# Convolution on 64x64 blocks of TensorE, in a sequence that mixes long and short blocks

## The chip, the cores and the metric

One core of one Trainium2 chip runs the whole program. The metric is the device time in microseconds (us) of one execution; the kernel before takes 877.8 us (median of 3 runs, 876.87 to 878.94).

## The reference, cut to what matters

The input `x` is [32 batches, 64 channels, 1024 features]. The program adds to it an attention block fed by a causal long convolution, and then a feed-forward block with low-rank experts. Only the convolution is touched, and the weights of the layer behind it:

```python
u_m    = u * mask                         # positions at or past length[batch] are zero
kernel = _get_kernel(log_dt, C, ...)      # [64 channels, 1024 positions]
y = irfft(rfft(u_m) * rfft(kernel))[..., :1024] + u_m * D
y = y * mask
# then q, k, v = y @ Wq.T, y @ Wk.T, y @ Wv.T ...
```

So for each channel, `y[b, t] = sum over s <= t of kernel[t - s] * x[b, s]`. The kernel of a channel comes from products of two small tables (a row index and a column index of 32 each), which TensorE forms in groups of eight channels.

## The kernel before, in words

**The convolution as matrix products.** The 1024 positions of a channel are 8 tiles of 128, or 16 blocks of 64. A row-shifted copy of the channel's kernel, the Toeplitz operand `toep`, lies with 64 partitions per channel and L + 64 = 1088 columns; any 64 of its columns are the 64x64 block that carries inputs over one distance. Two channels are worked on at once, one in partitions 0 to 63 and one in 64 to 127: a "pair", and there are 32 pairs (`for n in range(S // 2)` in `conv_matmuls`). The inputs of a pair, `xc`, hold for each tile the two 64-row halves; 32 batches are the columns, so a product over k tiles has 32k columns.

`convolve` (line 668) issues for each distance d in tiles and each input half c one product. `wide` (line 644) does it on the 64x128 form of the array: 64 rows of contraction, all 128 output positions, one instruction for each channel of the pair. `narrow` (line 655) does the same with two 64x64 products, one for each 64-row half of the output. Nine of sixteen (d, c) are wide in even pairs and eight in odd ones; wide and narrow runs are laid so that two narrow runs meet. In tile distance 0 the late input half also meets the early output half; that block of `toep` is all zero and is multiplied too. All operands are float32, for which each product shows as two records in the trace.

Products of a pair go to two PSUM banks of a ring of three pairs. VectorE multiplies them with the mask (line 740), ScalarE rounds to the high part `y_hi` (lines 771, 772), GpSimd subtracts for the low part `y_lo` (lines 783, 784).

**The loads.** The Toeplitz operand is read from the scratch `kpad` in DRAM by four DMAs for each pair (line 606: two channels, two halves of the columns) into a ring of three buffers. The load for pair n waits until pair n-3 has been multiplied (line 617), the inputs of pairs n, n+1 for the same (line 593, two DMAs every second pair, issued ahead of the Toeplitz loads). All of these sit in one in-order queue, SyncE's (`conv_loads`, line 625). In the same queue `conv_loads` puts one quarter of a weight block behind each of the loads of pairs 5 to 16: two blocks of the value weights and the first block of the key weights (line 642).

**The group kernels.** Every four pairs `kernels_pe` (line 536) makes the kernels of the eight channels of a later group: four 64x128 products of 128 columns. VectorE adds the two row halves (line 561 and following), ScalarE's queue stores them to `kpad` (line 573).

**The splits of the weights.** At pairs 15 and 19 ScalarE makes the high parts of the value weights and of the first key weights (line 820), and GpSimd their low parts at pairs 15, 19 and 23 (lines 824, 828).

**What follows.** The value products (line 952) come first; their first half needs only the first 16 pairs. Then the key and query products (line 988), attention, and the feed-forward block.

Of the kernel before, what the change touches and what calls it, by code (L numbers as in the profile page):

```python
# [14 lines left out]
P = 128  # L15
# [19 lines left out]
HB = 32  # L35
# [29 lines left out]
def constants():  # L65

    t = np.zeros((P, NCONST), np.float32)

    def put(name, v):
        at, n = CONSTS[name]  # L70
        t[:, at:at + n] = v

    p = np.arange(P)
    put("ident", np.eye(P))
    inv_freq = (1.0 / np.float32(10000.0) ** (np.arange(0, HD, 2, dtype=np.float32) / HD)).astype(np.float32)
    freqs = np.outer(np.arange(S, dtype=np.float32), inv_freq).astype(np.float32)
# [6 lines left out]
    put("pos", p[:, None] + P * np.arange(NJ)[None, :])  # L83
# [18 lines left out]
def build(nc, x_conv, x_nat, lens, cond, modes, d_skip,  # L102
          w_qk, w_v, w_o, w_cond, w_ffn, w_b, consts, out):
    ctx = ExitStack()
    with ctx:
# [26 lines left out]
        WR = 3  # L132
        W_FIRST = 6
        wraw = sb("wraw", [P, WR, NJ * P], F32, s12)
# [3 lines left out]
        TR = 3  # L138
        toep = sb("toep", [P, TR, L + HALF], F32, s1)
        XH, XR = 2, 2  # L140
# [409 lines left out]
        def kernels_out(v, g):  # L550
            v.wait_ge(pe_k, step_of(g) + 1)
            if g == 2:
                for pair in range(GP):
                    v.wait_ge(st_first[pair], 16 * 2)
            if g > 2:
                for pair in range(XH):
                    v.wait_ge(st_k[g % 2 * XH + pair], stored_before(g - 2))
            k = ksb[:, g % 2, :, :]
            low = ps[:, 6, 0:GC].rearrange("p (u b) -> p u b", u=2)
            high = ps[:, 7, 0:GC].rearrange("p (u b) -> p u b", u=2)  # L560
# [5 lines left out]
            v.tensor_tensor(k0, k0, along(d_at[:, g, :], GP), ALU.add).then_inc(v_k, 1)  # L566

        def store_kernels(eng, g):
            eng.wait_ge(v_k, step_of(g) + 1)
            heads = kpad.ap()[g * HGRP:(g + 1) * HGRP, P - 1:P - 1 + L].rearrange("(u k) (a b) -> k a u b", u=2, b=HB)  # L570
            for pair in range(XH):
                for k in (pair, XH + pair):
                    eng.dma_start(heads[k], ksb[k * HB:(k + 1) * HB, g % 2, :, k * HB:(k + 1) * HB])\
                       .then_inc(st_k[g % 2 * XH + pair], 16)
# [19 lines left out]

        FIRST_ROWS = [(0, 2 * P + HALF), (2 * P + HALF, NJ // 2 * P + HALF), (NJ // 2 * P + HALF, L + HALF)]

        ROW_HALVES = [(0, (L + HALF) // 2), ((L + HALF) // 2, L + HALF)]

# [6 lines left out]
        def load_rows(eng, n, r, lo, hi, landed):  # L605
            eng.dma_start(toep[r * HALF:(r + 1) * HALF, n % TR, lo:hi],  # L606
                          bass.AP(kpad, head(n, r) * (KROW + 1) + lo, [[1, HALF], [1, hi - lo]])).then_inc(landed, 16)

# [13 lines left out]
        W_PIECES = 4  # L622
        W_COLS = NJ * P // W_PIECES

        def conv_loads(sp):
# [4 lines left out]
            for n in range(1, S // 2):  # L630
# [6 lines left out]
                load_toeplitz(sp, n)  # L637
                part, piece = divmod(n - W_FIRST + 1, W_PIECES)
                if 0 <= part < 3:
                    cols = slice(piece * W_COLS, (piece + 1) * W_COLS)  # L640
                    source = w_v[:, part * NJ * P:(part + 1) * NJ * P] if part < 2 else w_qk[0]
                    sp.dma_start(wraw[:, part, cols], source[:, cols]).then_inc(ld_w[part // 2 * 2], 16)

        def wide(pe, n, c, d, start, stop=False):

            at = d * P + (1 - c) * HALF
            for r in range(2):
                rows = slice(r * HALF, (r + 1) * HALF)
                mm = pe.matmul(ps[:, 2 * (n % 3) + r, d * NB:NJ * NB], toep[rows, n % TR, at:at + P],  # L649
                               xc[rows, n // XH % XR, 1 - c, n % XH, 0:(NJ - d) * NB],  # L650
                               start=start, stop=stop)
            return mm

        def narrow(pe, n, c, d, start, stop=False):

            for half in range(2):
                at = d * P + (1 + half - c) * HALF
                for r in range(2):
                    rows = slice(r * HALF, (r + 1) * HALF)
                    mm = pe.matmul(ps[half * HALF:(half + 1) * HALF, 2 * (n % 3) + r, d * NB:NJ * NB], toep[rows, n % TR, at:at + HALF],  # L660
                                   xc[rows, n // XH % XR, 1 - c, n % XH, 0:(NJ - d) * NB],
                                   start=start, stop=stop)
            return mm

        TILES = [(d, c) for d in range(NJ) for c in range(2)]
        WIDE, NARROW = TILES[:NJ + 1], TILES[NJ + 1:]

        def convolve(pe, n):
# [6 lines left out]
            else:  # L675
                pe.wait_ge(ld_toep[n % TR], rows_landed(n))
            if n % 2 == 0:
                for d, c in WIDE:
                    if n == 0 and (d, c) == (2, 0):
                        pe.wait_ge(ld_mid, 16 * 2)  # L680
                    if n == 0 and (d, c) == (4, 0):
                        pe.wait_ge(ld_toep[0], 16 * 2)
                    mm = wide(pe, n, c, d, start=((d, c) == WIDE[0]))
                for d, c in NARROW:
                    mm = narrow(pe, n, c, d, start=False, stop=((d, c) == NARROW[-1]))
            else:
                for d, c in [WIDE[0]] + NARROW:
                    mm = narrow(pe, n, c, d, start=((d, c) == WIDE[0]))
                if n == 1:
                    kernels_pe(pe, 1)  # L690
                for d, c in WIDE[1:]:
                    mm = wide(pe, n, c, d, start=False, stop=((d, c) == WIDE[-1]))
            mm.then_inc(pe_conv, 1)
# [60 lines left out]
        def conv_hi(act):  # L754
# [4 lines left out]
            for n in range(S // 2):  # L759
# [4 lines left out]
                if n % GP == 0 and 0 < g < NHG - 1:  # L764
                    store_kernels(act, g + 1)
                if n == W_FIRST + 9:
                    weight_hi(act, -1)
                if n == W_FIRST + 13:
                    weight_hi(act, 0)
                act.wait_ge(v_mask, n + 1)  # L770
# [5 lines left out]
        def conv_lo(gp):  # L776
            exponents(gp, 1)
            for n in range(S // 2):
# [5 lines left out]
                gp.tensor_tensor(y_pair(1, n, 1), ym_pair(n, 1), y_pair(0, n, 1).bitcast(F32), ALU.subtract).then_inc(g_ylo, 1)  # L784
                if n == W_FIRST + 9:
                    value_weight_lo(gp, 0)
                if n == W_FIRST + 13:
                    value_weight_lo(gp, 1).then_inc(g_wlo, 1)
                if n == W_FIRST + 17:
                    weight_lo(gp, 0)  # L790

# [5 lines left out]
        def w_loaded(eng, m):  # L797

            s = w_slot(m).start
            pieces = (2 * W_PIECES, 0, W_PIECES)[s]  # L800
            whole = 0 if m <= 0 else (m - 1) // WR + 1 if s == 0 else m // WR + (s == 1)
            eng.wait_ge(ld_w[s], 16 * (pieces + whole))

# [4 lines left out]
        def load_weights(sp, m):  # L808
# [4 lines left out]
            s = w_slot(m).start  # L813
            sp.dma_start(wraw[:, s, :], w_qk[m]).then_inc(ld_w[s], 16)

# [67 lines left out]

        def qkv_transfers(sp):
            load_weights(sp, 1)
            load_weights(sp, 2)
# [115 lines left out]
        def qkv_hi(act):  # L1002
            act.wait_ge(g_ylo, S // 2)
            for n in range(4 * NU):
                if next_weights(n) is not None:
# [68 lines left out]

        def qkv_rope_sin(gp):
            for n in range(4 * NU):
                if next_weights(n) is not None:
# [836 lines left out]
```

## Time and profile before

| what | us |
|---|---|
| median of 3 runs | 877.8 |
| the profiled execution itself | 876.56 |
| its span | 874.7 |
| PE busy in it | 854.1 (98%) |
| products at line 649 (wide), busy | 97.1 |
| first product of the convolution starts | 20.55 |
| first value product starts | 164.40 |

The span is the time from the first to the last instruction; the profiled execution is 1.86 us longer than it. PE is TensorE's matmuls, PEld its weight loads, which run beside them. SPq is SyncE's queue while it issues DMAs. The granted clock is 1.00 in all 40 slices of the profile.

### The profile page before, as it was taken

What the parts mean: (1) busy time and instruction counts of PE and PEld (TensorE: products, weight loads), DVE (VectorE), ACT (ScalarE), POOL (GpSimd) and SP (SyncE); (2) the same over time, 40 slices, a digit from 0 to 9 for tenths busy, and PEclk for the clock granted to TensorE, in tenths of its full rate; (3) what the DMA queues carried; (4) which work ended last, traced back from release to release, by engine and by line L of the source; (5) the groups of instructions that cost most, each with busy time, mean ns of one, the idle gap of its engine ahead of it and who ended that gap; (6) DMA issues with size and microseconds to landing.
All of it is one profiled execution on the core that took longest, in us unless ns stands there. A gap on an engine that the chain in (4) does not pass through costs nothing.

```text
span 874.7 us, 24616 instructions
## 1 busy us (share of the span) xinstructions
PE 854.1 (98%) x10866; PEld 741.9 (85%) x10866; DVE 467.1 (53%) x898; ACT 221.4 (25%) x377; POOL 450.0 (51%) x346
## 2 busy tenths in 40 slices
PE   3999999999999999999999999999999999999998
PEld 2899999988888888887777777777779999999998
DVE  7555651122522222238887777888854755545444
ACT  4445552100000000013132333333334322211220
POOL 3344555302367555649978888877746422102220
PEclk9999999999999999999999999999999999999999
DMA  3788877413354322255534454545437211222211
GB/s 95 177 207 220 208 186 196 162 60 127 109 183 129 82 74 73 50 166 154 142 129 149 135 176 165 173 163 173 151 123 234 96 59 57 83 97 97 98 49 49
DMA packets 97339, 114.90 MB, mean 131 GB/s; under 512 B 44112, under 2 KB 66896, under 8 KB 97232
## 3 DMA queue, kind: packets, MB, share of 16 engines
q1 hardware_dynamic: 94240, 112.29, 43.1%
q8 instruction: 86, 1.41, 0.7%
q10 hardware_dynamic: 2480, 0.51, 0.3%
q0 software_dynamic: 512, 0.53, 0.2%
q14 instruction: 21, 0.17, 0.1%
HBM read 80.16 MB, written 33.13 MB: 130 GB/s over the span
## 4 chain that ended last, share of the span: by engine, by line
PE 93%; SPq 3%; DMA 2%; DVE 1%; issue 0%; ACT 0%
PE ps L988 25%; PE ps L1275 21%; PE ps L1597 15%; PE ps L649 8%; PE ps L1625 5%; PE ps L952 5%; PE ps L660 4%; PE ps L1231 3%; PE ps L1211 3%; PE ps L1507 2%; SPq L606 2%; DMA toep<-kpad 2%; PE ps L1642 1%; PE ps L1641 1%; DMA kpad<-ksb 1%
## 5 line engine op out<-in xcount | busy, mean ns | idle before, releaser
L1597 PE MATMUL ps<-wb_hi,xf 128*128 128x424 f32 x440 | 127.0, 356 | 0.0
L988 PE MATMUL ps<-y_hi,w_hi 128*128 128x512 f32 x320 | 125.1, 391 | 0.0
L988 PE MATMUL ps<-y_hi,w_lo 128*128 128x512 f32 x320 | 124.5, 389 | 0.0
L988 PE MATMUL ps<-y_lo,w_hi 128*128 128x512 f32 x320 | 124.5, 389 | 0.0
L1573 POOL TENSOR_TENSOR xf<-xs,xf 128x512 fp32r<-128x512 f32 x32 | 42.1, 1347 | 124.8 <-DVE xs L1561 124.8
L1275 PE MATMUL ps<-y_hi 128*128 128x512 f32 x256 | 102.9, 402 | 0.0
L1275 PE MATMUL ps<-y_hi,y_lo 128*128 128x512 f32 x256 | 100.2, 391 | 0.0
L1275 PE MATMUL ps<-y_lo,y_hi 128*128 128x512 f32 x256 | 100.1, 391 | 0.0
L649 PE MATMUL ps<-xc,toep 64*128 64x192 f32 (+4 forms) x1088 | 97.1, 330 | 2.5 <-DMA toep<-kpad 2.4
L649 PEld LDWEIGHTS ps<-xc,toep 64*128 64x128 f32 x1088 | 91.2, 187 | 6.0 <-issue 3.8
L1597 PEld LDWEIGHTS ps<-wb_hi,xf 128*128 128x128 f32 x440 | 82.7, 188 | 2.3
L1100 POOL TENSOR_TENSOR rot<-rot,cst 128x512 f32<-128x512 f32 x40 | 52.8, 1319 | 58.7 <-DVE rot L1070 58.7
L1303 POOL TENSOR_TENSOR sc<-sc,stat 128x1024 f32<-128x1024 f32 x32 | 62.0, 1937 | 38.8 <-DVE stat L1299 38.8
L1597 PE MATMUL ps<-wb_lo,xf 128*128 128x424 f32 x220 | 77.6, 353 | 0.0
L1070 DVE LOAD_MASK_SELECT rot<-ps x40 | 0.6, 14 | 134.1 <-PE ps L988 119.1
L988 PEld LDWEIGHTS ps<-y_hi,w_hi 128*128 128x128 f32 x320 | 60.1, 188 | 12.8
L988 PEld LDWEIGHTS ps<-y_hi,w_lo 128*128 128x128 f32 x320 | 60.1, 188 | 12.5
L988 PEld LDWEIGHTS ps<-y_lo,w_hi 128*128 128x128 f32 x320 | 60.1, 188 | 12.3
L1317 POOL TENSOR_TENSOR sc<-sc,stat 128x1024 f32<-128x1024 f32 x32 | 66.8, 2086 | 2.2 <-DVE stat L1313 2.2
L783 POOL TENSOR_TENSOR y_lo<-ym,y_hi 128x256 fp32r<-128x256 f32 x32 | 30.3, 946 | 70.0 <-ACT y_hi L772 69.8
L1104 POOL TENSOR_TENSOR rf<-rot,rc 128x512 f32<-128x512 f32 x40 | 52.7, 1317 | 17.2 <-DMA k_rows<-rf 14.1
L820 ACT ACTIVATE w_hi<-wraw 128x1024 fp32r<-128x1024 f32 (+1 forms) x11 | 12.4, 1137 | 186.6 <-PE ps L988 108.8
(190 smaller groups left out, 1624.3 us busy)
## 6 DMA issues: line engine op xcount, KB each, us to landing
toep<-kpad SPq DMA_DIRECT2D x124, 136.0 KB
xc<-in_dram SPq DMA_DIRECT2D x32, 256.0 KB, 4.4
q_rows<-rf SPq DMA_DIRECT2D x32, 256.0 KB, 2.8
q<-q_rows SPq DMA_DIRECT2D x16, 512.0 KB, 3.9
xr<-in_dram SPq DMA_DIRECT2D x16, 512.0 KB, 4.4
x_scratch<-xr SPq DMA_DIRECT2D x16, 512.0 KB, 3.0
x<-x_scratch SPq DMA_DIRECT2D x16, 512.0 KB, 4.3
out_dram<-x SPq DMA_DIRECT2D x15, 512.0 KB, 2.9
```

Of the source, the lines that this page charges most:

```text
L649: mm = pe.matmul(ps[:, 2 * (n % 3) + r, d * NB:NJ * NB], toep[rows, n % TR, at:at + P], xc[rows, n // XH % XR, 1 - c, n % XH, 0:(NJ - d) * ...
L660: mm = pe.matmul(ps[half * HALF:(half + 1) * HALF, 2 * (n % 3) + r, d * NB:NJ * NB], toep[rows, n % TR, at:at + HALF], xc[rows, n // XH % ...
L952: mm = pe.matmul(out, wv[a][:, j, h * P:(h + 1) * P], y[b][:, j, b0:b1, s0:s1], start=(j == 0 and a + b == 0), stop=(j == NJ - 1 and a == 1))
L988: mm = pe.matmul(kq_bank(n), w[a][:, j, :], yt[b][:, j, g * 512:(g + 1) * 512], start=(j == 0 and a + b == 0), stop=(j == NJ - 1 and a == 1))
L1100: gp.tensor_tensor(r, r, across(C("sin"), 8), ALU.mult).then_inc(g_rsin, 1)
L1104: gp.tensor_tensor(rf[:, (NVB + n) % SR, :], rot[:, n % RR, :], rc[:, n % RR, :], ALU.add).then_inc(g_rsum, 1)
L1275: mm = pe.matmul(ps[:, 6 + n, :], heads, wo(c, t)[:, n, :], start=(at == 0), stop=(at == 3 * NQT - 1))
L1303: gp.tensor_tensor(sc_groups(u), sc_groups(u), along(stat[:, u % CR, 0, :], S), ALU.subtract).then_inc(g_sub, 1)
L1317: gp.tensor_tensor(sc_groups(u), sc_groups(u), along(stat[:, u % CR, 2, :], S), ALU.mult).then_inc(g_prob, 1)
L1573: gp.tensor_tensor(xf(i, op, 1)[:], xs(i, op), xf(i, op, 0)[:].bitcast(F32), ALU.subtract).then_inc(g_xflo, 1)
L1597: mm = pe.matmul(dst[:, PLAIN:], xf(i, idx, a)[:, t, :], wb(c, idx, t), start=(start and t == 0 and a + c == 0), stop=(t == 3 and a == 1), ...
L1625: mm = pe.matmul(plain_bank[:, k, :], xf(i, op, a)[:, t, :], w[c][:, first + t, :], start=(op in (A11, S1) and t + a + c == 0), stop=(op i ...
```

## The change

- `toeplitz_block` takes the place of `wide` and `narrow`: every product is 64x64, with at most 128 columns. Output tiles 0 to 3 and 4 to 7 are separate segments (`seg`). In segment 1 the two 64-row halves of the output tiles are exchanged: `side` 0 holds the late half. A block is (side, segment, distance in 64s); the blocks of the zero corner are not issued. There are 46 blocks for each channel of a pair, in place of 9 wide and 14 narrow ones in even pairs, 8 wide and 16 narrow ones in odd pairs.
- The sequence of a pair is `MIXED_ORDER`: distance 0 of both segments, then for far = 1 to 7 the blocks of segment 1 at distance far (128 columns), of segment 0 at 8 - far and of segment 1 at 16 - far, and last distance 8. Pair 0 goes by rising distance.
- The Toeplitz operand has 1024 columns in place of 1088, and its loads accordingly.
- `kernels_pe` makes only the diagonal blocks that are used: eight 64x64 products of 64 columns, and VectorE's three operations on them are half as wide.
- The mask's positions and the weights' rows follow the exchanged halves: half of each weight block is loaded with its partition halves exchanged. A weight load in the layer behind is three DMAs in place of one.
- The value weights' first block is loaded in four pieces behind pairs 5, 8, 11, 14, its second in four pieces of two DMAs behind pairs 17, 20, 23, 26; they are split at pairs 27 and 29. The first key weights are loaded and split behind the convolution.

```diff
-        toep = sb("toep", [P, TR, L + HALF], F32, s1)
+        toep = sb("toep", [P, TR, L], F32, s1)
@@ kernels_pe
             for u in range(2):
-                cols = slice(u * P, (u + 1) * P)
-                for r in range(2):
-                    rows = slice(r * HALF, (r + 1) * HALF)
-                    mm = pe.matmul(ps[:, 6 + r, cols], ltab[rows, cols], rtab[rows, cols], start=True, stop=True)
+                for half in range(2):
+                    cols = slice(u * P + half * HALF, u * P + (half + 1) * HALF)
+                    for r in range(2):
+                        rows = slice(r * HALF, (r + 1) * HALF)
+                        mm = pe.matmul(ps[half * HALF:(half + 1) * HALF, 6 + r, u * HALF:(u + 1) * HALF], ltab[rows, cols], rtab[rows, cols],
+                                       start=True, stop=True)
@@ convolution
-        def wide(pe, n, c, d, start, stop=False):
-        def narrow(pe, n, c, d, start, stop=False):
+        def toeplitz_block(pe, n, at, start, stop):
+            side, seg, dist = at
+            late = side if seg == 0 else 1 - side
+            c = (late - dist) % 2
+            shift = (dist + c - late) // 2
+            lo, hi = max(seg * NJ // 2, shift), (seg + 1) * NJ // 2
             for r in range(2):
                 rows = slice(r * HALF, (r + 1) * HALF)
+                mm = pe.matmul(ps[side * HALF:(side + 1) * HALF, 2 * (n % 3) + r, lo * NB:hi * NB], toep[rows, n % TR, dist * HALF:(dist + 1) * HALF],
+                               xc[rows, n // XH % XR, 1 - c, n % XH, (lo - shift) * NB:(hi - shift) * NB],
                                start=start, stop=stop)
             return mm
+        def reach(side, seg):
+            return (seg + 1) * NJ - 2 + (side if seg == 0 else 1 - side)
+        def both_sides(seg, dist):
+            return [(side, seg, dist) for side in range(2) if dist <= reach(side, seg)]
+        BY_DISTANCE = [at for dist in range(NDIST) for seg in (1, 0) for at in both_sides(seg, dist)]
+        MIXED_ORDER = both_sides(1, 0) + both_sides(0, 0)
+        for far, small in zip(range(1, NJ), range(NJ - 1, 0, -1)):
+            MIXED_ORDER += both_sides(1, far) + both_sides(0, small) + both_sides(1, small + NJ)
+        MIXED_ORDER += both_sides(1, NJ)
@@ load_weights
-            sp.dma_start(wraw[:, s, :], w_qk[m]).then_inc(ld_w[s], 16)
+            near, far = slice(0, NJ // 2 * P), slice(NJ // 2 * P, NJ * P)
+            sp.dma_start(wraw[:, s, near], w_qk[m][:, near]).then_inc(ld_w[s], 16)
+            sp.dma_start(wraw[0:HALF, s, far], w_qk[m][HALF:P, far]).then_inc(ld_w[s], 16)
+            sp.dma_start(wraw[HALF:P, s, far], w_qk[m][0:HALF, far]).then_inc(ld_w[s], 16)
```

## Rows read from the trace of the kernel before

**Rows 1.** The page's first part: busy time, share, instructions of each engine.
```profile
PE 854.1 (98%) x10866; PEld 741.9 (85%) x10866; DVE 467.1 (53%) x898; ACT 221.4 (25%) x377; POOL 450.0 (51%) x346
```

**Rows 2.** Windows by stage: length, busy time by engine, granted clock, DMA share, GB/s.
```profile
36.20:95.00 58.80, 57.76 (x1268) 54.63 (x1261) 31.20 (x66) 30.63 (x51) 29.20 (x34) 1.00 0.91 218
95.00:164.40 69.40, 69.18 (x1522) 65.70 (x1521) 27.09 (x51) 27.43 (x47) 38.88 (x39) 1.00 0.72 187
```

**Rows 3.** The chain in order of time (start, length, what): two pairs in mid-convolution.
```profile
83.14 5.90 PE ps L649 x68
89.03 2.59 PE ps L660 x120
91.63 2.80 PE ps L649 x32
```

**Rows 4.** Windows over line 660 alone: length, PE busy (records), PEld, clock, DMA.
```profile
80.47:81.30 0.83, 0.82 (x40) 0.82 (x44) 1.00 1.08 235
80.47:81.51 1.04, 1.03 (x56) 1.03 (x60) 1.00 1.09 234
```

**Rows 5.** Groups by line and form: count, busy us, mean ns of one.
```profile
L660 PE MATMUL ps<-xc,toep 64*64 64x96 f32 x512 | 16.4, 243 | 0.0
...
L660 PE MATMUL ps<-xc,toep 64*64 64x64 f32 x512 | 13.2, 218 | 0.0
...
L660 PE MATMUL ps<-xc,toep 64*64 64x32 f32 x512 | 12.4, 212 | 0.0
```

**Rows 6.** The chain in order of time: three places where a Toeplitz load ends last.
```profile
27.92 3.83 DMA toep<-kpad
...
31.89 3.31 PE ps L649 x36
...
63.26 4.70 DMA toep<-kpad
...
138.44 0.63 SPq L593
...
139.83 0.55 SPq L606
...
141.71 5.21 DMA toep<-kpad
...
147.05 3.31 PE ps L649 x36
```

**Rows 7.** TensorE's timeline: pairs 3, 4 and 10, and their idle time before.
```profile
40.42 0.61 PE L543 MATMUL ps<-ph 64*128 64x128 f32 x8
41.14 3.31 PE L649 MATMUL ps<-xc,toep 64*128 64x256 f32 x36
...
55.40 2.87 PE L649 MATMUL ps<-xc,toep 64*128 64x256 f32 x32
...
68.09 3.31 PE L649 MATMUL ps<-xc,toep 64*128 64x256 f32 x36 [0.93 <-DMA toep<-kpad]
```

**Rows 8.** SyncE's timeline: issues in the convolution and behind it.
```profile
53.80 0.57 SPq L642 DMA_DIRECT2D wraw<-in_dram  x1
...
129.56 1.29 SPq L593 DMA_DIRECT2D xc<-in_dram  x2
130.95 6.86 SPq L606 DMA_DIRECT2D toep<-kpad  x8
```

**Rows 9.** GpSimd's timeline: a weight split, the last low parts, the first key split.
```profile
115.87 2.38 POOL L824 TENSOR_TENSOR w_lo<-wraw,w_hi 128x1024 fp32r<-128x1024 f32 x1
...
166.34 0.90 POOL L783 TENSOR_TENSOR y_lo<-ym,y_hi 128x256 fp32r<-128x256 f32 x1 [2.45 <-ACT y_hi L772]
167.18 0.91 POOL L784 TENSOR_TENSOR y_lo<-ym,y_hi 128x256 fp32r<-128x256 f32 x1
```

**Rows 10.** The whole chain in order of time: value products, key and query products.
```profile
164.40 44.37 PE ps L952 x240
208.77 179.52 PE ps L988 x792
```

More of the change, by code:

```diff
@@ L82, in constants @@
     put("causal", np.where(q < k, np.finfo(np.float32).min, np.float32(0)))
-    put("pos", p[:, None] + P * np.arange(NJ)[None, :])
+    turned = np.arange(NJ)[None, :] >= NJ // 2
+    put("pos", np.where(turned, (p[:, None] + HALF) % P, p[:, None]) + P * np.arange(NJ)[None, :])
     put("step", np.arange(HB)[None, :])
@@ L132, in build @@
         WR = 3
-        W_FIRST = 6
+        W_FIRST, W_EVERY = 5, 3
         wraw = sb("wraw", [P, WR, NJ * P], F32, s12)
@@ L557, in kernels_out @@
                     v.wait_ge(st_k[g % 2 * XH + pair], stored_before(g - 2))
-            k = ksb[:, g % 2, :, :]
-            low = ps[:, 6, 0:GC].rearrange("p (u b) -> p u b", u=2)
-            high = ps[:, 7, 0:GC].rearrange("p (u b) -> p u b", u=2)
+            k = ksb[:, g % 2, :, 0:HALF]
+            low = ps[:, 6, 0:P].rearrange("p (u b) -> p u b", u=2)
+            high = ps[:, 7, 0:P].rearrange("p (u b) -> p u b", u=2)
             v.tensor_copy(k, low).then_inc(v_kl, 1)
@@ L565, in kernels_out @@
             k0 = k.rearrange("p u (i b) -> p u i b", b=HB)[:, :, :, 0]
-            v.tensor_tensor(k0, k0, along(d_at[:, g, :], GP), ALU.add).then_inc(v_k, 1)
+            v.tensor_tensor(k0, k0, along(d_at[:, g, :], 2), ALU.add).then_inc(v_k, 1)
         def store_kernels(eng, g):
@@ L572, in store_kernels @@
                 for k in (pair, XH + pair):
-                    eng.dma_start(heads[k], ksb[k * HB:(k + 1) * HB, g % 2, :, k * HB:(k + 1) * HB])\
+                    eng.dma_start(heads[k], ksb[k * HB:(k + 1) * HB, g % 2, :, k % 2 * HB:(k % 2 + 1) * HB])\
                        .then_inc(st_k[g % 2 * XH + pair], 16)
@@ L593, in load_x_conv @@
                 sp.dma_start(xc[r * HALF:(r + 1) * HALF, t % XR, :, :, :], halves[:, :, first:first + XH, :]).then_inc(ld_xc[t % XR], 16)
-        FIRST_ROWS = [(0, 2 * P + HALF), (2 * P + HALF, NJ // 2 * P + HALF), (NJ // 2 * P + HALF, L + HALF)]
-        ROW_HALVES = [(0, (L + HALF) // 2), ((L + HALF) // 2, L + HALF)]
+        FIRST_ROWS = [(0, 2 * P), (2 * P, NJ // 2 * P), (NJ // 2 * P, L)]
+        ROW_HALVES = [(0, L // 2), (L // 2, L)]
         def rows_landed(n):
@@ L623, in build @@
         W_COLS = NJ * P // W_PIECES
+        W_SPLIT = 27
         def conv_loads(sp):
@@ L637, in conv_loads @@
                 load_toeplitz(sp, n)
-                part, piece = divmod(n - W_FIRST + 1, W_PIECES)
-                if 0 <= part < 3:
+                part, piece = divmod((n - W_FIRST) // W_EVERY, W_PIECES)
+                if n >= W_FIRST and (n - W_FIRST) % W_EVERY == 0 and part < 2:
                     cols = slice(piece * W_COLS, (piece + 1) * W_COLS)
-                    source = w_v[:, part * NJ * P:(part + 1) * NJ * P] if part < 2 else w_qk[0]
-                    sp.dma_start(wraw[:, part, cols], source[:, cols]).then_inc(ld_w[part // 2 * 2], 16)
@@ L644, in wide @@
-        def wide(pe, n, c, d, start, stop=False):
-            at = d * P + (1 - c) * HALF
+                    rows = w_v[:, part * NJ * P:(part + 1) * NJ * P]
+                    if part == 0:
+                        sp.dma_start(wraw[:, 0, cols], rows[:, cols]).then_inc(ld_w[0], 16)
+                    else:
+                        sp.dma_start(wraw[0:HALF, 1, cols], rows[HALF:P, cols]).then_inc(ld_w[0], 16)
+                        sp.dma_start(wraw[HALF:P, 1, cols], rows[0:HALF, cols]).then_inc(ld_w[0], 16)
@@ L651, in wide @@
                                start=start, stop=stop)
             return mm
-        def narrow(pe, n, c, d, start, stop=False):
[L656 to L663, printed above, removed]
@@ L665, in build @@
-        TILES = [(d, c) for d in range(NJ) for c in range(2)]
-        WIDE, NARROW = TILES[:NJ + 1], TILES[NJ + 1:]
+        NDIST = 2 * NJ
+        def reach(side, seg):
[4 more added lines that the diff above has]
+        MIXED_ORDER = both_sides(1, 0) + both_sides(0, 0)
@@ L676, in convolve @@
                 pe.wait_ge(ld_toep[n % TR], rows_landed(n))
[L677 to L689, printed above, removed]
+            order = BY_DISTANCE if n == 0 else MIXED_ORDER
+            for k, at in enumerate(order):
+                if n == 0 and at == (0, 1, 4):
+                    pe.wait_ge(ld_mid, 16 * 2)
+                if n == 0 and at == (0, 1, 8):
+                    pe.wait_ge(ld_toep[0], 16 * 2)
+                if n == 1 and k == len(order) // 2:
                     kernels_pe(pe, 1)
-                for d, c in WIDE[1:]:
-                    mm = wide(pe, n, c, d, start=False, stop=((d, c) == WIDE[-1]))
+                last = all(other[0] != at[0] for other in order[k + 1:])
+                mm = toeplitz_block(pe, n, at, start=(at[1:] == (1, 0)), stop=last)
             mm.then_inc(pe_conv, 1)
@@ L765, in conv_hi @@
                     store_kernels(act, g + 1)
-                if n == W_FIRST + 9:
+                if n == W_SPLIT:
                     weight_hi(act, -1)
-                if n == W_FIRST + 13:
-                    weight_hi(act, 0)
                 act.wait_ge(v_mask, n + 1)
@@ L784, in conv_lo @@
                 gp.tensor_tensor(y_pair(1, n, 1), ym_pair(n, 1), y_pair(0, n, 1).bitcast(F32), ALU.subtract).then_inc(g_ylo, 1)
-                if n == W_FIRST + 9:
+                if n == W_SPLIT:
                     value_weight_lo(gp, 0)
-                if n == W_FIRST + 13:
+                if n == W_SPLIT + 2:
                     value_weight_lo(gp, 1).then_inc(g_wlo, 1)
-                if n == W_FIRST + 17:
-                    weight_lo(gp, 0)
         NU = NG + NQT
@@ L799, in w_loaded @@
             s = w_slot(m).start
-            pieces = (2 * W_PIECES, 0, W_PIECES)[s]
-            whole = 0 if m <= 0 else (m - 1) // WR + 1 if s == 0 else m // WR + (s == 1)
-            eng.wait_ge(ld_w[s], 16 * (pieces + whole))
+            pieces = 3 * W_PIECES if s == 0 else 0
+            whole = 0 if m < 0 else (m - 1) // WR + 1 if s == 0 else m // WR + 1
+            eng.wait_ge(ld_w[s], 16 * (pieces + 3 * whole))
         def w_users(m):
@@ L884, in qkv_transfers @@
         def qkv_transfers(sp):
+            load_weights(sp, 0)
             load_weights(sp, 1)
@@ L1003, in qkv_hi @@
             act.wait_ge(g_ylo, S // 2)
+            weight_hi(act, 0)
             for n in range(4 * NU):
@@ L1075, in qkv_rope_sin @@
         def qkv_rope_sin(gp):
+            weight_lo(gp, 0)
             for n in range(4 * NU):
```

4 lines of the change are left out of this document (1 added, 3 removed).

## The prediction

> **What bounds the kernel now.** Read the page's first part first: TensorE is busy 98% of the span [rows 1], no other engine over 53%. Then the chain in order of time: the value, key and query products stand in it unbroken for 44.37 and 179.52 us [rows 10], so nothing but their own length sets that stage. The change doesn't touch them; what it can win or lose lies before 164.40, where the first value product starts. There TensorE is busy for 57.76 of 58.80 and 69.18 of 69.40 us [rows 2], so the convolution is bound by its products. But the chain shows a second candidate close behind: in three places it runs through the Toeplitz loads (3.83, 4.70, 5.21 us from the last issue to the landing) [rows 6], and TensorE sat idle 0.93 us before pair 10 [rows 7]. The DMA share is 0.91 at 218 GB/s up to 95 us [rows 2]. So two limits lie within a few per cent of each other, and the sum has to be made for both.
>
> **The change, part by part.**
>
> *Length of a pair, before.* Two pairs are one wide run of 68 records (5.90 us) and one narrow run of 120 (2.59 us): 8.49, that is 4.245 us a pair [rows 3]. Columns: wide, even pair 2x256 + 2x224 + 2x192 + 2x160 + 128 = 1792, odd 256 less, 3328 for both; narrow 512 and 768, 1280 for both. That is 2304 a pair. A record streams a column in about 0.83 ns: the 64x96 record is 25 ns longer than the 64x64 one [rows 5], 0.78 ns a column, and two cycles at 2.4 GHz (granted clock 1.00, the upper level, in all stretches [rows 2]) are 0.83. With two records for a product: 2304 x 1.667 = 3.84 us. The other 0.405 us is overhead: changing between the 64x128 and the 64x64 form, a little at each round, and short rounds.
>
> *Length of a pair, after.* Both sides of the array have 2176 columns (side 0: 10x128 + 2x96 + 2x64 + 2x32 = 1664 in segment 1 and 512 in segment 0; side 1: 1536 and 640). So 2176 x 1.667 = 3.63 us. Records a pair: 46 x 2 channels x 2 = 184, before 94 on average (34 wide and 60 narrow).
> The price of more records is read from one narrow run [rows 4]. Its first 40 records (10 rounds of four: 128, 128, 4x96, 4x64 columns, 896 in all) took 0.83 us against 0.747 by columns; part of the 0.08 is the entry. Rounds down to 64 columns thus cost little over their columns. The next 16 records (four rounds of 32 columns) took 0.21 us, 52 ns a round against 27 by columns. Rows 5 say the same: from 64 to 32 columns the record shortens by 6 ns only. So a long round hides the next weight load and a 32-column round doesn't.
> Now the bounds. Below: 46 rounds' worth at 2.5 ns each is 0.12, nothing else, 3.75 us. Above: if the two sides have to go in step, each group costs its wider side, 2304 columns again, 3.84 + 0.12, and its eight 32-column rounds cost 25 ns more each, 0.20: 4.16. The old overhead by round gives about the same: 0.405 us over 32 rounds is 12.7 ns, by 46 rounds 0.58, so 4.21. I take 3.9: the sequence puts at most four short rounds behind two long ones, which is the pattern that was cheap, and no form is changed any more; the sides' differences (32 against 64, then 64 against 32) mostly meet again in the next group.
> The Trainium skill speaks to this twice, and the pages differ. "TensorEngine Tiling (Array Packing)", Key Properties, has tiles operate independently and a mode switch drain the array, which gives the low end. "TensorE: Matmul & The Clock Gate", Part 3, says matmuls start and end strictly in program order; two sides of unequal width would then wait for each other, which gives the upper figure (rival B). No run of before has unequal sides, so the trace decides neither.
>
> *Group kernels.* 8 records of 0.61 us with the neighbours' overlap, between the pairs [rows 7]; after, half the columns in each quadrant: about 0.3 us. Per four pairs that is 0.3 less on TensorE, if TensorE is the limit. VectorE's narrower additions save nothing: its share is 0.53 [rows 2].
>
> *The load path.* The load for pair n may start when pair n-3 is done. For even n, SyncE issues two input loads (1.29 us) and four Toeplitz loads at about 0.64 each [rows 8]; the last of these is issued 3.3 us after the end of pair n-3, and lands 3.83 to 5.21 us on [rows 6]: 7.2 to 8.6 us, with 0.14 to the start. Measured whole at pair 28: 138.44 to 147.05, 8.6 us; at pair 10, with the queue behind on weight pieces, 58.3 to 68.09, 9.8 us [rows 6, 7]. For odd n the 1.3 us of inputs fall away, so they aren't the limit. Call it L. If an even pair waits for its load, then start(n) = end(n-3) + L, the pair n-4 starts two pair lengths before end(n-3), and four pairs take 2T + L. With T = 4.245 that was 8.49 + 8.2 = 16.7 against 4T + 0.5 = 17.5: the load path was hidden. With T = 3.9 it is 7.8 + 8.2 = 16.0 against 4T + 0.3 = 15.9: the two limits meet, and the load path is the next wait. I take L = 8.2, above the middle, since the transfers come more densely: a pair moves 0.79 MB of operands (0.82 before), and with kernels and weights some 0.85 MB in 4.0 us, 212 GB/s, where before had 218 at a share of 0.91 [rows 2].
> The weights help a little: eight groups of pieces over 22 pairs in place of twelve behind pairs 5 to 16; each piece costs SyncE 0.57 us [rows 8]. Behind pairs 17, 20, 23, 26 two pieces are 1.2 us; the odd pair's load behind it has more room than that.
>
> *The start.* Pair 2 starts at 31.89 on a load that SyncE's queue set [rows 6], not the products; that stays. Pair 4 started at 41.14 [rows 7]; now two pairs and the kernels later 31.89 + 7.8 + 0.3 = 40.0, its own load at about 40.4. I take 40.4.
>
> *The end of the convolution.* GpSimd splits value weights behind pair 29: 2.38 us [rows 9]. Low parts end 3.7 us after their pair (167.18 + 0.91 against 164.40), so this split ends 6.1 us after pair 29's end, 1.7 before the value products begin at 7.8; pair 30's low part comes 0.4 us late, pair 31's not at all. Cost nothing; if ScalarE were late with the high part, up to 2 us. Behind the value products' 44.37 us [rows 10] there is room for loading and splitting the first key weights (three DMAs, about 2 us of issue). The two DMAs more in each later weight load are 1.3 us of SyncE for four products of 5.4 us; the chain there holds no load at all [rows 10].
>
> *The sum.* Pairs 4 to 31 are 28 pairs of 16.0/4 = 4.0 us: 40.4 + 112 = 152.4. The value products start 12.0 us earlier, and the rest follows unchanged. The profiled execution's 876.56 becomes 864.6. It stood 1.2 under the median of 877.8, so the median to expect is 865.8.
>
> **The rivals.**
> B, *the sides go in step*: T = 4.16, four pairs max(8.3 + 8.2, 16.6 + 0.3) = 16.9, the 28 pairs 118.5; the start at 40.6 gives 159.1, 5.3 us gained: 872.5. For it: nothing in the trace shows unequal sides at the same time. Against it: the wide runs keep going while the two channels are skewed, so strictly common rounds aren't needed there.
> A, *the load path takes it back*: L = 9.8 as at pair 10 [rows 7]; four pairs 17.6, the 28 pairs 123: 163.6, so 877.0. For it: a DMA share of 0.91 where L was longest [rows 2]. Against: the pair 10 case had a weight piece behind every pair, and total bytes fall.
> C, *slower: weight loads come bare*. If the mixture breaks the hiding and each round pays the 25 ns of a 32-column round [rows 4], T = 3.63 + 46 x 0.0275 = 4.9; 28 pairs are 139.3, to 180 us: 893. It decides from T = 4.35 on, 15 ns a round. For it: twice the records. Against it: the ten long rounds of rows 4 paid 8 ns at most, the entry included, and only 8 of 46 groups have 32 columns.
> D, *the exchange of the halves gains no column* (2304 after all, but short rounds as cheap as in the forecast): T = 3.84 + 0.12 = 3.96, four pairs 16.1, 28 pairs 113: 866.7. It lies inside the forecast's range, because the load path is the limit by then.
>
> **How the numbers follow.** The forecast's mechanism (T from 3.75 to 4.0, L from 7.5 to 8.6; 859 to 869) has 0.68; B 0.13, D 0.01 beyond the forecast's own values; A 0.12, of which most ends between 869 and 876; C 0.04; a new wait behind the convolution 0.02. The low end, T = 3.75 and L = 7.3: four pairs 15.3, 107 us, 147.4: 860.8; a little below that for an L under 7.2. The range that leaves out 2 in 10 is 860.5 to 872.5. A change of under 0.2% (1.8 us) can't be told from none. Faster than that: 0.93; within: 0.03; slower: 0.04.
>
> **What would show it.** The wide form gone; records at the new line 32x184 = 5888 in number; pair starts 3.9 to 4.0 apart; TensorE's idle time before even pairs grown from a few tenths to some us in all, released by the Toeplitz loads; the first value product at 152.4; the 44.37 and 179.5 us behind it unchanged. I am wrong if the records run without idle time at over 4.1 us a pair (B, C), if idle time takes over 10 us (A), or if idle time appears behind the convolution.

## The result, and the profile after

The changed kernel takes 934.9 us (median of 4 runs, 933.3 to 939.6) against 878.4 us: 1.0655 times as long, 95% interval 1.0625 to 1.0686. The forecast was 865.8, range 860.5 to 872.5. It was wrong in sign.

The profiled execution has a span of 932.0 us. Its page, first the busy time of each engine (before: [rows 1]), then TensorE's busy tenths in 40 slices, then the queue by which instructions arrive:

```profile
span 932.0 us, 30510 instructions
PE 860.3 (92%) x13802; PEld 746.9 (80%) x13802; DVE 466.6 (50%) x898; ACT 221.4 (24%) x377; POOL 449.1 (48%) x346
...
PE   3776776679999999999999999999999999999998
...
q8 instruction: 109, 1.79, 0.8%
```

TensorE has 2936 more matmul records and only 6.2 us more of busy time. Its share is 6 or 7 tenths in slices 1 to 8, where it was 9. The last row (packets, MB, share of 16 engines) is the one to learn to read: 109 packets, 1.79 MB, so 16.4 KB each. The program has 2 x 13802 matmuls and weight loads; 27604 by 109 is 253, so one packet is a block of about 256 instructions, 128 records with their weight loads. The same row of the kernel before:

```profile
q8 instruction: 86, 1.41, 0.7%
```

The row doesn't name the engine that a packet is for, but the difference does: the counts of the other engines hardly moved, and 2936 more TensorE records came with 23 more packets, 128 records for each.

And the same queue in the window from 20 to 165 us alone, in the convolution, of the kernel before and then of the changed one:

```profile
q8 instruction: 25, 0.41, 1.3%
```

```profile
q8 instruction: 34, 0.56, 1.7%
```

One block per 5.8 us before, one per 4.26 us after: 145 us by 25 and by 34. The packet itself is short: 1.7% of 16 engines in 145 us is 39 us for 34 packets, an estimate of 1.2 us for each.

Where the idle time is, and what ended it: the waits of TensorE in the convolution (idle us, times, longest), then its timeline from pair 4 on (start, length, what, records, idle before).

```profile
PE ps L661 <- issue: 52.9, 43, 2.2
PE ps L661 <- DMA toep<-kpad: 0.3, 1, 0.3
```

```profile
45.96 2.85 PE L661 MATMUL ps<-xc,toep 64*64 64x128 f32 x128 [0.34 <-issue]
50.51 3.11 PE L661 MATMUL ps<-xc,toep 64*64 64x96 f32 x127 [1.70 <-issue]
54.44 3.28 PE L661 MATMUL ps<-xc,toep 64*64 64x128 f32 x128 [0.82 <-issue]
58.65 2.96 PE L661 MATMUL ps<-xc,toep 64*64 64x32 f32 x128 [0.93 <-issue]
63.75 3.04 PE L661 MATMUL ps<-xc,toep 64*64 64x128 f32 x127 [2.14 <-issue]
```

Nothing that the profile shows was waited for ("issue"), the operand loads were in time (0.3 us in all), and the stops come every 128 records nearly throughout (43 stops; the convolution has 46 times 128 records), whatever block of the sequence stands there: before a product of 128, 96 or 32 columns, in the middle of a pair. A pair has 184 records, so these stops don't belong to pairs; the work between two of them is that of one packet of instructions.

The trace also has the start and the length of each packet of this queue, and they tie the two together. Each of the 43 stops ended 1.2 to 1.7 us (median 1.46) after such a packet had landed, and the next packet started 1.0 to 2.6 us (median 1.74) after TensorE had resumed; the packet itself took 1.1 us. 1.46 + 1.74 + 1.11 is 4.3 us: a chain of one packet at a time, not a full transfer path.

The whole convolution (count, shortest, median and longest record, first and last start):

```profile
L661 PE MATMUL ps<-xc,toep x5888: 186/269/471, 20.9 to 220.2; 64*64 64x128 f32 x91, 64*64 64x32 f32 x37, 64*64 64x96 f32 x35, 64*64 64x64 f32 x34
```

With the 112 records of the group kernels that is 6000 records in 199.3 us: 4.25 us for 128. Per pair 6.2 us, where the forecast had 4.0.

Behind it the chain in order of time answers [rows 10]:

```profile
220.49 44.34 PE ps L960 x240
264.84 179.52 PE ps L996 x792
```

The value products start 56.1 us later than before (220.49 against 164.40), and the lengths of both stages are the same. The span grew by 57.3 us; the other 1.2 us lie in the attention, where the chain shows two more stops released by nothing shown ("issue", 0.37 us at 536.0 and 0.75 at 639.7); the interval from tile to tile, 7.4 us elsewhere, is 8.2 and 8.4 there, and the kernel before had two smaller ones of this sort.

### The profile page after: what moved, and what is told of

Its sections match the earlier page's. It is cut to its first block, busy times and chain, and to the rows that moved or that the text cites. A ratio compares the mean times of both kernels' runs of the same rounds, so it can differ in the third digit from the quotient of the medians.

```text
span 932.0 us, 30510 instructions
## 1 busy us (share of the span) xinstructions
PE 860.3 (92%) x13802; PEld 746.9 (80%) x13802; DVE 466.6 (50%) x898; ACT 221.4 (24%) x377; POOL 449.1 (48%) x346
## 3 DMA queue, kind: packets, MB, share of 16 engines
q8 instruction: 109, 1.79, 0.8%
## 4 chain that ended last, share of the span: by engine, by line
PE 91%; issue 6%; DVE 1%; DMA 1%; SPq 1%; ACT 0%
PE ps L996 23%; PE ps L1285 19%; PE ps L661 15%; PE ps L1607 14%; PE ps L1635 5%; PE ps L960 5%; PE ps L1241 3%; PE ps L1221 3%; PE ps L1517 2%; PE ps L1652 1%; PE ps L1651 1%; SPq L609 1%; DMA kpad<-ksb 1%; DMA toep<-kpad 0%; PE ps L1619 0%
## 5 line engine op out<-in xcount | busy, mean ns | idle before, releaser
L661 PE MATMUL ps<-xc,toep 64*64 64x128 f32 (+3 forms) x5888 | 146.3, 253 | 53.2 <-issue 52.9
L661 PEld LDWEIGHTS ps<-xc,toep 64*64 64x64 f32 x5888 | 137.1, 138 | 61.6 <-issue 61.6
L748 DVE TENSOR_TENSOR ym<-ps,valid 128x512 f32<-128x512 f32 x32 | 22.1, 692 | 125.0 <-PE ps L661 124.9
```

The source lines that it names most:

```text
L661: mm = pe.matmul(ps[side * HALF:(side + 1) * HALF, 2 * (n % 3) + r, lo * NB:hi * NB], toep[rows, n % TR, dist * HALF:(dist + 1) * HALF], x ...
```

## The experiments

Two theories. **F**: TensorE is fed its instructions in blocks of 256, one about every 4.3 us at best, and 184 records a pair ask for more. **S**: the sequence is itself slow, by bare weight loads, by sides that wait for each other, or by the order. The kernel before ran beside all of them (877 to 879 us).

**Same count, fewer columns.** In the changed kernel:

```diff
             lo, hi = max(seg * NJ // 2, shift), (seg + 1) * NJ // 2
+            if dist > 0:
+                lo = hi - 1
```

> The changed kernel with every 64x64 product but those of distance 0 cut to its last 32 columns: the same 184 records a pair, about a third of the columns (the rest of the convolution's sum is left out). Theory F (TensorE is fed one 16 KB block of instructions, 128 records with their weight loads, about every 4.3 us): the count decides, so the convolution keeps 46 blocks x 4.3 = about 200 us and the run 925 to 937 us. Theory S (the products themselves, or weight loads laid bare, are slower in the mixed sequence): the convolution falls to the floor of short rounds, 46 rounds x 2 x 0.058 = 2.7 us of work a pair, then bound by the loads at about 4 us: 860 to 870 us.

Measured: 933.1 us. The products of this run, in the same view:

```profile
L663 PE MATMUL ps<-xc,toep x5888: 186/291/473, 20.9 to 219.6; 64*64 64x32 f32 x181, 64*64 64x128 f32 x16
```

And the granted clock by slices of its page:

```profile
PEclk9776777559999999999999999999999999999999
```

Of the 4352 columns of a pair (both sides) 1856 are left, 57% went, and the convolution is 0.6 us shorter: 4.24 us for 128 records. The time goes with the count, not with the columns. The run is less clean than it looks, since the granted clock was lower in most of this stretch (0.50 to 0.83 by windows of 20 us) and the records took longer for it; but TensorE still stood for 44.6 us in 32 stops that nothing shown released, and each ended 1.3 to 1.7 us after an instruction packet had landed. Together with the bare length of a pair further down, S is out as the cause of the 56 us.

**No Toeplitz loads** from pair 3 on:

```diff
-                load_toeplitz(sp, n)
+                if n < TR:
+                    load_toeplitz(sp, n)
+                else:
+                    sp.wait_ge(pe_conv, n - TR + 1)
```

> The changed kernel with no Toeplitz loads from pair 3 on; the products read the three buffers that are there (so the convolution's values are those of the first three pairs' kernels). Two thirds of the stage's DMA bytes go. Theory F1 (the instruction blocks queue behind data on the shared DMA engines): a block comes every 2.5 to 3.5 us, the convolution gets 30 to 70 us shorter: 865 to 905 us. Theory F2 (the rate of the blocks is a latency of its own, whatever the traffic): about 4.2 us a block, 925 to 935 us. Theory L (a load path of the operands is the limit): 865 or less.

Measured: 918.9 us. The same 6000 records lie between 20.3 and 205.3 us: 3.95 us for 128. The DMA traffic from 20 to 165 us is 66 GB/s in place of 141, and a block of instructions comes only 0.30 us sooner. Neither of the two figures expected was met exactly, but F2 is the nearer.

**Almost no operand bytes.** The same, and the inputs from pair 4 on cut:

```diff
+                if t < XR:
                     sp.dma_start(xc[r * HALF:(r + 1) * HALF, t % XR, :, :, :], halves[:, :, first:first + XH, :]).then_inc(ld_xc[t % XR], 16)
+                else:
+                    sp.dma_start(xc[r * HALF:(r + 1) * HALF, t % XR, 0, :, 0:NB], halves[:, 0, first:first + XH, 0:NB]).then_inc(ld_xc[t % XR], 16)
```

> The changed kernel without Toeplitz loads from pair 3 on, as in the run before with 4.0 us a block, and with the input loads from pair 4 on cut to one input half and one tile (the convolution's values are no longer the reference's): almost no operand bytes on the DMA engines. If traffic is what is left above a fixed latency, a block of instructions comes every 3.5 to 3.8 us, 895 to 912 us in all. If 3.9 to 4.0 us is the floor: 915 to 920 us.

Measured: 914.6 us; 26 GB/s, 180.3 us for the 6000 records, 3.85 us for 128. So of the 4.25 us some 0.4 go with the traffic, and 3.85 remain with hardly anything beside them (one run each). It lies between the two floors that I had named. In this run a stop ended 1.38 us after a packet's landing, the next packet started 1.25 us after that, and a packet took 1.17 us (medians of 46 stops): 3.8 us. What went with the traffic is mostly the time up to the next packet's start, 1.74 us in the changed kernel. Why the next packet starts no earlier isn't shown.

**Half the channels.** The second channel of each pair left out but for distance 0 and the closing blocks:

```diff
-            for r in range(2):
+            for r in (range(2) if dist == 0 or stop else range(1)):
```

> The changed kernel with the second channel of each pair left out but for distance 0 and the closing blocks: 104 records a pair in place of 184, the columns of the first channel's two quadrants unchanged. Theory F: 104/128 x 4.3 = 3.5 us a pair, under the products' own 3.75 to 3.9, so idle time for instructions all but goes, and the forecast's two limits hold: about 4.0 a pair, 860 to 872 us. Theory S: the pair's length is set by the sides' own sequence and stays near 6.2 us: over 915 us.

Measured: 934.7 us, which at first sight speaks for S. The windows (length, busy by engine, granted clock, DMA share, GB/s) show why it doesn't:

```profile
100.00:140.00 40.00, 38.26 (x991) 37.44 (x988) 21.20 (x50) 20.29 (x35) 19.95 (x25) 1.00 0.76 196
140.00:180.00 40.00, 38.45 (x580) 38.24 (x578) 8.87 (x18) 9.86 (x17) 10.78 (x12) 0.57 0.51 131
```

In most stretches the granted clock was near its lower level (0.5 of full), with half of the array's rows unused in most of the products. Where it stood at 1.00, TensorE made 991 records in 40 us, 9.5 pairs of 104: 4.2 us a pair, near the 4.0 of F and far from the 6.2 of S. Its matmuls never waited for instructions in the convolution, its weight loads for 6.2 us. The total decides nothing; this kernel changed the clock together with the count.

**Long blocks only**, which cuts the count without emptying half of the array (`full` is true for a block of 128 columns; the shorter ones are left out):

```diff
+        MIXED_ORDER = [at for at in MIXED_ORDER if full(at)]
```

> The changed kernel with all blocks of under 128 columns left out from pair 1 on: 22 blocks, 88 records a pair, the loads as they are. Theory F: 88/128 x 4.3 = 3.0 us a pair for instructions, 2.4 to 2.5 us of products; then the load path of the forecast is what is left, four pairs 2T + L = 5.0 + 8.2, that is 3.3 a pair (or 3.7 with L = 9.8): 840 to 858 us. A rival in which something else in the stage, other than the records' number, costs the 6.2 us a pair: over 880 us.

Measured: 864.3 us, a little over the range and far under the rival's. The waits of TensorE in this convolution, and the windows from pair 4 to its end:

```profile
PE ps L661 <- DMA toep<-kpad: 24.4, 15, 3.4
PE ps L661 <- issue: 7.8, 9, 2.0
```

```profile
41.60:152.00 110.40, 83.11 (x2544) 78.62 (x2544) 52.79 (x109) 55.19 (x92) 60.70 (x67) 0.92 0.79 204
```

With 88 records a pair the wait for instructions falls from 52.9 to 7.8 us, and the load path comes out behind it: 15 waits, 24.4 us. 28 pairs in some 110.4 us are 3.94 us a pair, at products of 2.35 by their columns (22 rounds of 128 columns, two records, 0.833 ns a column). What holds the loads is SyncE's own queue: its waits from 41 to 152 us for pairs to be done (us, times, longest), and its Toeplitz issues there (shortest, median, longest, in ns):

```profile
SPq L596 <- PE ps L661: 1.6, 2, 1.0
SPq L620 <- PE ps L661: 0.5, 1, 0.5
```

```profile
L609 SPq DMA_DIRECT2D toep<-kpad x104: 444/597/1584, 42.1 to 145.4; - x104
```

It hardly waits for a pair to be done, it issues nearly all the time: 95.5 of the 105 us from 41 to 146, and of the rest 2.3 us are gaps of over 0.3 us. Eight Toeplitz loads of 0.68 us on average, two input loads of 0.70 and a share of the weights, with the gaps between them, are 7.9 us for two pairs. So with these DMAs the queue comes to about 3.9 us a pair, however short the products. Whether its longer issues are held up by the traffic isn't shown.

**The bare length of a pair.** TensorE waits ahead of each pair, so that its instructions can arrive:

```diff
+            if n > 3:
+                pe.wait_ge(g_ylo, n)
```

> The changed kernel, and TensorE waits ahead of each pair from 4 on until the low parts of the pair before are made (3.7 us behind its end). In that time the instruction store can fill, so that a pair's 184 records run without waiting for instructions; the bare length T of a pair in the new sequence can be read from its start to its end. Theory F: T is 3.75 to 4.2 us, and the whole hardly moves, since the added wait of 3.7 us a pair covers the wait for instructions of about 2.2 (some 940 to 970 us in all). Theory S (the sequence itself is slow): T is 5 us or more, and the run over 975 us.

Measured: 1039.6 us, 70 over F's range, and by the total alone what S had named (over 975). But the granted clock fell in most pairs, with 3.5 to 4.2 us of idle time ahead of each. Two pairs ran at 1.00 (4.22 and 4.23 us in the timeline), and the timeline of the first of them reads:

```profile
160.85 4.22 PE L661 MATMUL ps<-xc,toep 64*64 64x128 f32 x184 [3.92 <-POOL y_lo L792]
164.86 0.44 PE L545 MATMUL ps<-ph 64*64 64x64 f32 x16
```

The windows over this pair and the next one (length, busy by engine, granted clock, DMA share, GB/s):

```profile
160.80:165.10 4.30, 4.25 (x200) 4.28 (x200) 0.00 (x0) 0.00 (x0) 0.00 (x0) 1.00 0.22 61
169.00:174.90 5.90, 5.86 (x184) 5.61 (x184) 0.00 (x0) 0.00 (x0) 0.88 (x2) 0.71 0.34 86
```

In the first window 184 records stand without a stop, from 160.85 to the next work at 164.86: T is 4.0 us. In the second the clock was 0.71, and the pair took 5.9. So the total is the clock's, and T at full clock is what the run was made for: not S's 5 or more. The 4.0 is inside the forecast's bounds (3.75 to 4.21) and 0.25 under the 4.245 of before.

**Order by distance** for all pairs:

```diff
-            order = BY_DISTANCE if n == 0 else MIXED_ORDER
+            order = BY_DISTANCE
```

> The changed kernel with all pairs in the order of rising distance, the short blocks in one run at the end: the same 184 records. Theory F: the order doesn't matter, 928 to 940 us. Theory S (the mixture of long and short lays the weight loads bare): clearly another time, 20 us or more away.

Measured: 930.8 us, 4.20 us for 128 records. The order of the blocks is worth some 4 us at most here, and with one run not even that is sure.

**Fewer, undivided 64x64 products** in the kernel before (31 blocks, up to 256 columns, 124 records a pair, group kernels as changed):

```diff
+                mm = pe.matmul(ps[side * HALF:(side + 1) * HALF, 2 * (n % 3) + r, d * NB:NJ * NB], toep[rows, n % TR, (dist + 1) * HALF:(dist + 2) * HALF],
+                               xc[rows, n // XH % XR, 1 - c, n % XH, 0:(NJ - d) * NB],
+                               start=start, stop=stop)
...
+        MERGED = sides(0)
+        for dist in range(1, NJ):
+            MERGED += sides(dist) + sides(2 * NJ - dist)
+        MERGED += sides(NJ)
```

> The kernel before with all products in the 64x64 form, undivided up to 256 columns: 31 blocks, 124 records a pair in place of 184 (and of 94 before), the zero block left out but the sides uneven (2048 and 2304 columns); the group kernels as in the changed kernel. Theory F: 124/128 x 4.34 = 4.2 us a pair, above or at the products' own 4.0 to 4.1: the convolution takes 134 to 139 us against 144 before, 872 to 878 us. Theory S, by which 64x64 products in a mixed sequence are slow: 10 us or more slower than before.

Measured: 886.0 us, 1.0106 times the kernel before (1.0084 to 1.0127), slower where I expected a small gain. Its timeline:

```profile
49.48 4.34 PE L673 MATMUL ps<-xc,toep 64*64 64x256 f32 x128 [1.11 <-issue]
54.35 8.26 PE L673 MATMUL ps<-xc,toep 64*64 64x256 f32 x239 [0.54 <-issue]
...
141.19 12.89 PE L673 MATMUL ps<-xc,toep 64*64 64x128 f32 x384 [0.91 <-issue]
```

The longest stretch without a stop, 384 records in 12.89 us, gives about 4.1 us a pair, so one block of instructions is needed every 4.2 us; the supply of the changed kernel was one in 4.25, and still 128 records took 4.75 us over the whole convolution (151.5 us from its first to its last record, 143.6 in the kernel before). The stops come singly (10.0 us in 15 waits with those of the group kernels), with loads that also end late (4.0 us in three waits). So a need just at the edge of this supply, which varies, costs more than the ratio of the two averages; that part of F I had left out.

**All products wide**, long and short alternating, in the kernel before (64 records a pair):

```diff
+        ALTERNATE = [TILES[0]]
+        for near, far in zip(TILES[1:NJ], TILES[:NJ:-1]):
+            ALTERNATE += [near, far]
+        ALTERNATE += [TILES[NJ]]
```

> The kernel before with all sixteen products of a pair in the 64x128 form, long and short alternating: 64 records a pair in place of 94, 2304 columns as before, no change of form. Theory F: half as many instruction blocks as before, never the limit; a pair takes 3.84 + 0.1 to 0.3 us, so 3.95 to 4.15, and the load path's 2T + 8.2 for four pairs gives 4.03 to 4.1 a pair against 4.4 before: 867 to 872 us. Rival (the loads of 128 columns of weights are bare behind short products, which is why narrow ones were there): 4.3 to 4.5 a pair, 878 to 884 us.

Measured: 884.5 us, 1.0080 times before (1.0051 to 1.0109): the rival. Groups by form (busy, mean ns):

```profile
L649 PE MATMUL ps<-xc,toep 64*128 64x224 f32 x256 | 40.0, 389 | 0.0
...
L649 PE MATMUL ps<-xc,toep 64*128 64x32 f32 x256 | 21.5, 232 | 0.0
```

And TensorE's timeline over four pairs:

```profile
97.36 0.64 PE L543 MATMUL ps<-ph 64*128 64x128 f32 x8
97.81 18.60 PE L649 MATMUL ps<-xc,toep 64*128 64x256 f32 x256
116.21 0.64 PE L543 MATMUL ps<-ph 64*128 64x128 f32 x8
```

Four pairs take 18.40 us (97.81 to 116.21) without idle time, 4.60 each; by their columns they would be 3.84. The 224-column record next to a 32-column one takes 389 ns, where among its like it took 349 in the kernel before, and a 32-column record, 27 ns by its columns, takes 232. That fits weight loads of 128 columns that short neighbours don't hide, as the rival said. No run has all products wide in descending order, so how much of the loss is the alternation and how much the short wide products isn't separated; against this version the narrow products of the kernel before earn their place.

**Two pairs of four undivided**, the others as before (109 records a pair):

```diff
+            if n % 4 in (1, 2) and n > 1:
+                for k, (side, dist) in enumerate(MERGED):
+                    last = all(other != side for other, _ in MERGED[k + 1:])
+                    mm = merged_block(pe, n, side, dist, start=(dist == 0), stop=last)
```

> The kernel before, with pairs 1 and 2 of every four (from pair 2 on) made of 31 undivided 64x64 blocks, pairs 0 and 3 as before: one run of the 64x128 form and one of the 64x64 form in four pairs in place of two of each, 109 records a pair on average, 368 of them in one 64x64 run of about 10.6 us. Theory F: the store holds 256 records' instructions, so such a run needs one block of instructions while it lasts, which takes 4.3 us and fits; the four pairs fall from 17.4 us by 0.5 us (two changes of form less): 873 to 877 us. If the blocks of instructions are asked for only when one is used up and the short stretches don't average out: 879 to 883 us, slower.

Measured: 880.2 us, 1.0029 (1.0014 to 1.0044): slower by a little, as the second of the two expectations had it. Four pairs without a wait took 17.15 us, group kernels included, 0.3 less than before. TensorE waited 1.6 us for instructions, where before had none, and 4.4 us for loads (before 3.3); these waits take the gain back.

**The weights' new schedule alone** in the kernel before:

```diff
-        W_FIRST = 6
+        W_FIRST, W_EVERY = 5, 3
+        W_SPLIT = 27
```

> The kernel before with nothing but the new schedule of the weights: value weights behind pairs 5 to 26, split at 27 and 29, first key weights behind the convolution. By all theories the rest of the change is not what costs 56 us. I expect the 0.9 us stall before pair 10 to go and nothing to come behind the convolution: 876 to 878.5 us, 0 to 2 us faster. If the schedule is at fault somewhere: slower by 1 us or more.

Measured: 876.3 us, 0.9991 (0.9973 to 1.0009). No difference that can be told, so the schedule isn't what costs the 56 us. TensorE's waits for loads did not shrink as expected: 4.0 us in all, before 3.3.

No version that computes the whole result was faster than the kernel before by more than the noise.

## Why the prediction was wrong, by its steps

- **The step that failed** is "the price of more records is read from one narrow run". It priced a record by the time it holds the array, in a run of 56 records. That price was right; the term that was left out is the supply: 184 records a pair are 1.44 blocks of instructions, at 4.25 us 6.1 us, against products of 4.0. Neither A, B, C nor D has this mechanism. C has the sign right, but for another reason: its bare weight loads would make a pair 4.9 us long, and the one that ran without a stop took 4.0.
- The clue stood in the profile of before: the instruction queue at one block per 5.8 us, and 3.8 us of "issue" waits in the weight loads of the wide products. The change asks for a block every 2.8 us (128 of 184 records in 4.0 us), twice the rate that any long stretch before it had shown; that bound the forecast should have drawn.
- The Trainium skill has the matter, in "Runtime: NRT & Kernel Launch", Instruction fetch mechanics: instructions stream from memory in blocks of 16 KiB, 256 instructions, fetched while the current block runs. The packets of 16.4 KB and the stops every 128 records agree, and so does the next packet's start after TensorE had gone on. The Trainium skill also says there that the fetch is hidden because dispatch is slower than the fill; the measured 52.9 us of stops say otherwise for short products in four quadrants, and the measurement decides.
- **Length of a pair**: forecast 3.9, bounds 3.75 to 4.21; measured 4.0. Right. Whether the sides wait for each other is not settled by it: 4.0 fits 2176 columns and some bare short rounds as well as 2304 columns. The 2.5 ns a round of the lower bound comes from no row; rows 4 give 8 ns, and (4.0 - 3.63) over 46 rounds is 8 ns again.
- **Load path**: forecast four pairs 2T + L with L = 8.2, so 4.0 us a pair at T = 3.9. In the long-blocks run this formula gives 3.3 and 3.94 was measured. The formula lets SyncE wait for the end of pair n-3 before it issues, and in that run it waited for pairs 2.1 us in all: what holds the loads is the length of its issues, 7.9 us for two pairs, which the forecast had in its rows but never added up over two pairs (for even pairs it took 0.64 us an issue, where rows 8 have 6.86 us for eight). That this lands beside the forecast's 4.0 is luck. In the changed kernel neither counted, since TensorE waited 0.3 us for loads.
- **The start**: pair 4 starts at about 45.0 us, forecast 40.4; its first stops for instructions are there already.
- **The end of the convolution**: nothing behind it; 44.34 and 179.52 us stand unchanged, and the schedule of the weights alone measured 0.9991. Right.
- **Group kernels**: 16 records in 0.44 us in place of 8 in 0.61. Right and without weight.
- The forecast named idle time of over 10 us as its refutation, released by loads. It was 52.9 us, and what released it was in no row of the waits; it took the packets' own times to see it. "Issue" deserves to be read as a resource.

## What to carry to other kernels

Before cutting products into smaller ones, divide: matmul records per us in the new sequence against what TensorE was fed in this case at best, 128 records (256 instructions with the weight loads) in 3.85 to 4.25 us, some 30 to 33 a us. The kernel before ran at 22 a us, the changed one asked for 46. Stay clear of the edge as well: at some 30 a us, the undivided 64x64 products, the stage was still 5% longer than before. Read the instruction queue's row of a profile with the same care as the data queues'. And add up the issues of a DMA queue over a whole period before you model it as waiting for anything.

## What the runs showed of the hardware that was not expected

- A block of instructions for TensorE came every 4.25 us with 141 GB/s of other traffic, 3.95 at 66 and 3.85 at 26: less than a tenth of it goes with the traffic.
- In the changed kernel TensorE resumed 1.2 to 1.7 us after an instruction packet of 16.4 KB had landed, and the next packet started 1.0 to 2.6 us after that (43 stops).
- SyncE's queue took 0.68 us on average for a Toeplitz load of 128 KB and 0.70 for an input load of 256 KB, and with four and one of them a pair and the weights it was full at 3.94 us a pair.
- The granted clock fell to its lower level with one channel's quadrants left out (0.57 in a stretch in which TensorE was busy for 38.45 of 40 us), and with waits of 3.5 to 4.2 us between pairs.
- In the 64x128 form an alternation of long and short products made a pair 4.6 us long, where its columns take 3.84; with the short products made narrow and run together, as in the kernel before, it is 4.245.
